# Boundary samples of a modulated convolution chain in three chunks of 43, 43 and 42, in place of four of 32

## The reference, cut to what matters

```python
# x: 128 samples, 64 channels, 1024 positions; style: 128 x 128
for i, typ in enumerate(('same', 'upsample', 'same', 'downsample')):
    s = style @ mod_w[i].T + mod_b[i]
    weight = SCALE * weights[i] * s[:, None, :, None]
    weight = weight * rsqrt(sum(weight**2, over input channels and taps) + EPS)
    # 'same': 3 taps; 'upsample': transposed conv by 2, then the blur 1,3,3,1;
    # 'downsample': the blur, then a conv with stride 2
    out = layer(out, weight, biases[i])
return x + out
```

## Time and profile before

| | us |
|---|---|
| median of 3 runs | 667.52 |
| lowest and highest of the 3 | 664.25, 668.52 |
| the profiled execution | 665.44 |
| its span, first to last instruction | 663.6 |
| mean granted TensorE clock | 0.987 |

### The profile page before, as it was taken

How to read it: one execution, slowest core, us unless ns; L and a number is a source line. 1 busy time by engine, 2 the same in 40 slices (tenths; PEclk the granted TensorE clock), 3 DMA queues, 4 the chain that set the end, 5 groups by cost and what they waited for, 6 DMA issues and landing times.

```text
span 663.6 us, 13288 instructions
## 1 busy us (share of the span) xinstructions
PE 624.9 (94%) x5012; PEld 618.6 (93%) x5012; DVE 534.0 (80%) x800; ACT 431.7 (65%) x713; POOL 230.8 (35%) x246
## 2 busy tenths in 40 slices
PE   5557999999999999999999999999999999999977
PEld 4546999999999999999999999999999999999977
DVE  6898687888888788798888787797888878887941
ACT  3416577686677677776777767666677777666553
POOL 4314324432333333422333344324323343234230
PEclk9988999999999999999999999999999999999989
DMA  5125577767788877777788777777977778778872
GB/s 191 61 63 136 153 205 191 216 200 208 202 213 239 216 182 223 205 196 211 203 232 218 185 220 218 206 192 203 239 197 197 224 209 217 203 189 236 216 197 108
DMA packets 155839, 129.75 MB, mean 196 GB/s; under 512 B 7104, under 2 KB 122304, under 8 KB 155776
## 3 DMA queue, kind: packets, MB, share of 16 engines
q1 hardware_dynamic: 155120, 127.33, 71.2%
q10 hardware_dynamic: 656, 1.57, 0.7%
HBM read 36.41 MB, written 33.75 MB: 106 GB/s over the span
## 4 chain that ended last, share of the span: by engine, by line
PE 76%; DVE 13%; issue 4%; ACT 4%; DMA 1%; POOL 0%; ACTq 0%; DVEq 0%; POOLq 0%
PE py L169 10%; PE py L170 10%; PE py L168 10%; PE pg L168 6%; PE pg L169 6%; PE pg L170 6%; PE ps L168 6%; PE ps L169 6%; PE ps L170 6%; PE pg L173 3%; PE pg L174 3%; DVE pg L667 1%; DVE xl L659 1%; DMA T<-in_a 1%; DVE Q2l L690 1%
## 5 line engine op out<-in xcount | busy, mean ns | idle before, releaser
L169 PE MATMUL py<-xl,W 128*128 128x256 f32 x640 | 182.7, 285 | 0.0
L170 PE MATMUL py<-xh,W 128*128 128x256 f32 x640 | 182.4, 285 | 0.0
L168 PE MATMUL py<-xh,W 128*128 128x256 f32 x640 | 182.1, 285 | 0.1
L614 POOL TENSOR_TENSOR X<-X 128x514 f32<-128x514 f32 x64 | 73.5, 1149 | 218.3 <-DMA X<-in_xin 216.0
L168 PEld LDWEIGHTS py<-xh,W 128*128 128x128 f32 x640 | 127.2, 199 | 0.3 <-ACT py L449 0.3
L170 PEld LDWEIGHTS py<-xh,W 128*128 128x128 f32 x640 | 127.1, 199 | 0.0
L169 PEld LDWEIGHTS py<-xl,W 128*128 128x128 f32 x640 | 126.5, 198 | 0.0
L659 DVE TENSOR_TENSOR xl<-X,xh 128x1548 fp32r<-128x1548 f32 x64 | 114.1, 1782 | 8.7 <-ACT xh L443 8.2
L449 ACT COPY py<-ps 128x512 f32<-128x512 f32 x128 | 73.4, 573 | 69.2 <-PE ps L170 68.8
L168 PE MATMUL ps<-xh,W 128*128 128x256 f32 x384 | 109.6, 285 | 4.2 <-issue 1.9
L169 PE MATMUL ps<-xl,W 128*128 128x256 f32 x384 | 109.2, 284 | 0.0
(11 more groups left out here) (164 smaller groups left out, 1449.9 us busy)
## 6 DMA issues: line engine op xcount, KB each, us to landing
X<-in_xin SPq DMA_DIRECT2D x64, 516.0 KB, 5.4
out<-T SPq DMA_DIRECT2D x64, 512.0 KB, 3.5
W<-W SPq DMA_DIRECT2D x64, 384.0 KB, 4.4
W<-W SPq DMA_DIRECT2D x96, 128.0 KB, 4.3
W<-M SPq DMA_DIRECT2D x96, 128.0 KB, 3.6
W<-W SPq DMA_DIRECT2D x32, 256.0 KB, 4.7
E<-in_ed ACTq DMA_DIRECT2D x1, 768.0 KB, 8.5
XE<-in_xe SPq DMA_DIRECT2D x1, 512.0 KB, 4.8
```

The costliest lines, as they stand in the source:

```text
L168: eng.matmul(o, wh_, rh, start=first, stop=False, skip_group_check=onto)
L169: eng.matmul(o, wh_, rl, start=False, stop=False, skip_group_check=onto)
L170: return eng.matmul(o, wl_, rh, start=False, stop=last, skip_group_check=onto)
L614: pool.tensor_tensor(x[:, :, 3, 0:XW - 1], x[:, :, 0, 1:XW], x[:, :, 1, 0:XW - 1], ALU.subtract)
```

## The change

The chunk size goes from 32 to 43. `chunk(c)` gives the samples of a chunk, 43, 43 and 42, and `NCH` = 3 the number of chunks. Every edge instruction on PE and DVE takes only the first `n` (or `m`) samples of its buffers, which have grown with `EC`. The steps stand in the same places, k-th step of chunk c in groups 8c + 2k and 8c + 2k + 1; groups 24 to 31 now have none.

```diff
-EC = 32
+EC = 43
+def chunk(c):
+    return min(EC, B - c * EC)
+NCH = -(-B // EC)
...
-            sp.wait_ge(s_ed, 5 * (B // EC))
+            sp.wait_ge(s_ed, 5 * NCH)
...
             def edge(c, k):
+                n = chunk(c)
                 pe.wait_ge(s_ed, 5 * c + k + 1)
                 if k == 0:
                     for t in range(3):
-                        m = pe.matmul(pe_[:, 0:6 * EC], E[:, 0, t, :], XS[:, :, t:t + 6], start=t == 0, stop=t == 2)
+                        i = pe.matmul(pe_[:, 0:6 * n], E[:, 0, t, :], XS[:, 0:n, t:t + 6], start=t == 0, stop=t == 2)
...
-                if i == 3 and g % 2 == 0:
+                if i == 3 and g % 2 == 0 and g < 8 * NCH:
                     edge(*divmod(g // 2, 4))
...
-                    link(dve.tensor_scalar(Y[:, :, 1:12], v, BB[:, 0, 1:2], None, ALU.add))
-                    link(tt(Y1[:, :, 0:11], Y[:, :, 1:12], Y[:, :, 0:11], ALU.add))
+                    link(dve.tensor_scalar(Y[:, 0:m, 1:12], v, BB[:, 0, 1:2], None, ALU.add))
+                    link(tt(Y1[:, 0:m, 0:11], Y[:, 0:m, 1:12], Y[:, 0:m, 0:11], ALU.add))
...
-                if i == 2 and g % 2 == 1:
+                if i == 2 and g % 2 == 1 and g < 8 * NCH:
                     c, k = divmod(g // 2, 4)
                     edge(c, k)
-                    if k == 3 and c + 1 < B // EC:
+                    if k == 3 and c + 1 < NCH:
                         edge_in(c + 1)
```

More of the change, by code:

```diff
@@ L359, in edge @@
                     for t in range(3):
-                        m = pe.matmul(pe_[:, 0:6 * EC], E[:, 0, t, :], XS[:, :, t:t + 6], start=t == 0, stop=t == 2)
+                        i = pe.matmul(pe_[:, 0:6 * n], E[:, 0, t, :], XS[:, 0:n, t:t + 6], start=t == 0, stop=t == 2)
                 elif k == 1:
-                    pe.matmul(pe_[:, 0:6 * EC], E[:, 1, 0, :], ZE[:, :, 1:7], start=True, stop=False)
-                    pe.matmul(pe_[:, 0:6 * EC], E[:, 1, 2, :], ZE[:, :, 0:6], start=False, stop=True)
-                    m = pe.matmul(pe_[:, 6 * EC:11 * EC], E[:, 1, 1, :], ZE[:, :, 1:6], start=True, stop=True)
+                    pe.matmul(pe_[:, 0:6 * n], E[:, 1, 0, :], ZE[:, 0:n, 1:7], start=True, stop=False)
+                    pe.matmul(pe_[:, 0:6 * n], E[:, 1, 2, :], ZE[:, 0:n, 0:6], start=False, stop=True)
+                    i = pe.matmul(pe_[:, 6 * n:11 * n], E[:, 1, 1, :], ZE[:, 0:n, 1:6], start=True, stop=True)
                 elif k == 2:
                     for t in range(3):
-                        m = pe.matmul(pe_[:, 0:8 * EC], E[:, 2, t, :], U[:, :, t:t + 8], start=t == 0, stop=t == 2)
+                        i = pe.matmul(pe_[:, 0:8 * n], E[:, 2, t, :], U[:, 0:n, t:t + 8], start=t == 0, stop=t == 2)
                 else:
                     for t in range(3):
-                        m = pe.matmul(pe_[:, 0:3 * EC], E[:, 3, t, :], XB[:, :, t:t + 5:2], start=t == 0, stop=t == 2)
-                m.then_inc(s_e, 1)
+                        i = pe.matmul(pe_[:, 0:3 * n], E[:, 3, t, :], XB[:, 0:n, t:t + 5:2], start=t == 0, stop=t == 2)
+                i.then_inc(s_e, 1)
             for n in ("mwt", "st"):
@@ L719, in edge_in @@
             def edge_in(c):
-                cs = slice(c * EC, (c + 1) * EC)
-                tt(XS, XE[:, cs, :], bc(S[:, 0, cs], 8), ALU.mult).then_inc(s_ed, 1)
+                m = chunk(c)
+                cs = slice(c * EC, c * EC + m)
+                tt(XS[:, 0:m], XE[:, cs, :], bc(S[:, 0, cs], 8), ALU.mult).then_inc(s_ed, 1)
             def edge(c, k):
-                cs = slice(c * EC, (c + 1) * EC)
+                m = chunk(c)
+                cs = slice(c * EC, c * EC + m)
                 dve.wait_ge(s_e, 4 * c + k + 1)
-                got = lambda a, n: pe_[:, a * EC:(a + n) * EC].rearrange("p (b n) -> p b n", n=n)
+                got = lambda a, n: pe_[:, a * m:(a + n) * m].rearrange("p (b n) -> p b n", n=n)
@@ L727, in edge @@
                 if k == 0:
-                    v = Y1[:, :, 0:6]
+                    v = Y1[:, 0:m, 0:6]
                     link(tt(v, got(0, 6), bc(b0z[:, cs], 6), ALU.add))
-                    tt(ZE[:, :, 1:7], v, bc(D10[:, cs], 6), ALU.mult).then_inc(s_ed, 1)
+                    tt(ZE[:, 0:m, 1:7], v, bc(D10[:, cs], 6), ALU.mult).then_inc(s_ed, 1)
                 elif k == 1:
-                    v = Y1[:, :, 0:11]
+                    v = Y1[:, 0:m, 0:11]
                     tt(v[:, :, 0:11:2], got(0, 6), bc(S[:, 1, cs], 6), ALU.mult)
@@ L734, in edge @@
                     link(tt(v[:, :, 1:10:2], got(6, 5), bc(S[:, 1, cs], 5), ALU.mult))
-                    link(dve.tensor_scalar(Y[:, :, 1:12], v, BB[:, 0, 1:2], None, ALU.add))
-                    link(tt(Y1[:, :, 0:11], Y[:, :, 1:12], Y[:, :, 0:11], ALU.add))
-                    link(tt(Y2[:, :, 0:10], Y1[:, :, 1:11], Y1[:, :, 0:10], ALU.add))
-                    link(tt(Y1[:, :, 0:9], Y2[:, :, 1:10], Y2[:, :, 0:9], ALU.add))
-                    dve.scalar_tensor_tensor(out=U[:, :, 1:10], in0=Y1[:, :, 0:9], scalar=0.25, in1=bc(S[:, 2, cs], 9),
+                    link(dve.tensor_scalar(Y[:, 0:m, 1:12], v, BB[:, 0, 1:2], None, ALU.add))
@@ L740, in edge @@
+                    link(tt(Y1[:, 0:m, 0:11], Y[:, 0:m, 1:12], Y[:, 0:m, 0:11], ALU.add))
+                    link(tt(Y2[:, 0:m, 0:10], Y1[:, 0:m, 1:11], Y1[:, 0:m, 0:10], ALU.add))
+                    link(tt(Y1[:, 0:m, 0:9], Y2[:, 0:m, 1:10], Y2[:, 0:m, 0:9], ALU.add))
+                    dve.scalar_tensor_tensor(out=U[:, 0:m, 1:10], in0=Y1[:, 0:m, 0:9], scalar=0.25, in1=bc(S[:, 2, cs], 9),
                                              op0=ALU.mult, op1=ALU.mult).then_inc(s_ed, 1)
                 elif k == 2:
-                    v = Y1[:, :, 0:8]
+                    v = Y1[:, 0:m, 0:8]
@@ L743, in edge @@
                     link(tt(v, got(0, 8), bc(DD[:, 2, cs], 8), ALU.mult))
[L744 to L748, removed]
+                    link(dve.tensor_scalar(HH[:, 0:m, 2:10], v, BB[:, 0, 2:3], None, ALU.add))
@@ L749, in edge @@
+                    link(tt(Y1[:, 0:m, 0:9], HH[:, 0:m, 1:10], HH[:, 0:m, 0:9], ALU.add))
+                    link(tt(Y2[:, 0:m, 0:8], Y1[:, 0:m, 1:9], Y1[:, 0:m, 0:8], ALU.add))
+                    link(tt(Y1[:, 0:m, 0:7], Y2[:, 0:m, 1:8], Y2[:, 0:m, 0:7], ALU.add))
+                    dve.scalar_tensor_tensor(out=XB[:, 0:m], in0=Y1[:, 0:m, 0:7], scalar=0.125, in1=bc(S[:, 3, cs], 7),
                                              op0=ALU.mult, op1=ALU.mult).then_inc(s_ed, 1)
                 else:
-                    v = Y1[:, :, 0:3]
+                    v = Y1[:, 0:m, 0:3]
```

## The result

The changed kernel takes 669.42 us in the median of 20 runs (667.74 to 672.20), the kernel before 666.05 us in 20 runs (664.25 to 668.52). The ratio is 1.0047, with a 95% interval from 1.0037 to 1.0058: by this ratio slower by 3.1 us, between 2.5 and 3.9 (the two medians are 3.4 us apart). The forecast was +1.7 us with a range of 665.0 to 672.0, and "within 1%" as by far the likeliest case. The direction and the class held; the sum came out too small, above the +0.7 to +2.7 us that had 72 in 100.

What follows compares the result with a forecast made beforehand. PE was taken to bound the kernel, DVE costing only where PE waits. PE 0.0, DVE +1.7 and the last part 0 gave +1.7 us, stated as 668.6 us, range 665.0 to 672.0.

Steps and rivals of the forecast that it cites:

- Any time beyond some 2.3 us goes fully to PE: Behind k = 1 and k = 2 steps on DVE: 2.3 us is free room, the rest delays PE one for one.
- growth less the removed wait: DVE's part: k = 1 and k = 2 grow 2.65 us together, less 0.92 for group 27's k = 1 step: +1.73 us.
- the growth of the k = 1 steps of 43 samples: On DVE, 11 more samples add 0.70 us at most, taken as 0.51 since part hides in a wait for POOL.
- the sentence that named it: Odd 43 rows may cost line 735 its double rate: 0.1 us more for each of two k = 1 steps.
- PE's own part: PE's edge steps: k = 0, 1, 2 keep 12.7 us, k = 3 stays 0.66 at its floor; 0.0 us, at most -0.1.
- k = 0 and k = 3 on DVE: These DVE steps stay inside the free room of 2.3 us; k = 3 grows 0.16 and nothing shows.
- The middle of the last part: PE's removed late k = 2 step (1.29 us) shifts it before the `x_low` wait; up to 1.29 lost or 0.85 won, taken as 0.
- the rival in which this step is lost: Last part: `x_low` stays where it is, so the moved k = 2 step gains nothing; +3.0 us, 670; 12 in 100.
- The rival in which fewer instructions win: DVE's 18 removed instructions save 2.8 us of fixed parts; growth hides behind POOL; -1.8 us, 666 or below; 9 in 100.
- Neither buys anything: Last part: PE's k = 3 step in group 30 and DVE's in group 31 lie beside SP's chain; removing them gains nothing.
- one of the prediction's own signs of being wrong: Wrong if the time from 606 us on, less the moved step, changes by over 1.5 us.
- The rival of the falling clock: Longer waits behind k = 1, perhaps k = 2, drop PE to 1.2 GHz: +7 us (674) or +12 us (679); 5 in 100.

Runs made afterwards that it cites:

- the split kernels: DVE's steps k = 1 and k = 2 each cut in two: kernel before (chunks of 32) 661.15 us, 0.9916; changed kernel (43, 43, 42) 661.90 us, 0.9929.
- The 44-row run: Changed kernel with only the tensor_scalar instructions of lines 744 and 753 on 44 rows where a chunk has 43; one run, 667.74 us.
- the kernel without the last step: Kernel before without its very last edge step (k = 3 of the fourth chunk, groups 30 and 31); ratio 0.9998 to before.
- the filler: Changed kernel plus four fp32 matmuls of 336 columns on PE in group 30, results unread; 668.72 us, 1.0035 to before, and 1.0035 when repeated.
- the two shortened ones: Kernel before without its very last edge step, 0.9998 to before; and kernel before without its whole fourth chunk of edge steps, 0.9945.
- the fourth-chunk one: Changed kernel with a fourth chunk of 42 in groups 24 to 31, computing the third chunk's samples twice; 1.0116 to before.
- other k = 3 steps: Changed kernel with PE's k = 3 step reading adjacent columns in group 6, unchanged in 14, 96 columns in 22; one run, 669.65 us.
- the three with a filler: Changed kernel with four extra matmuls in group 30, twice, 1.0035 each; kernel before with DVE steps cut in two plus four 256-column matmuls, 659.85 us, 0.9910.

## Why the prediction was right or wrong

- **Waits behind the steps: right in kind, sized somewhat small.** "Any time beyond some 2.3 us goes fully to PE" held in each of the steps and was used backwards by the split kernels, to 0.1 us. The forecast was 1.43, 1.43 and 1.38 us behind k = 1, measured 1.61, 1.56 and 1.30; and 0.91, 0.91, 0.88 behind k = 2, measured 1.00, 0.90, 0.90. The sum of growth less the removed wait was to be 1.73 us and is 0.74 + 1.27 = 2.01.
- **The term that was mis-sized** is the growth of the k = 1 steps of 43 samples: 0.51 us in the sum, measured 0.69 and 0.65 (the step holds DVE 3.90 us for 3.21 and 3.25), close to the upper end of 0.70 that the prediction took down. It took 0.13 off because line 735 would wait for POOL and hide the growth of lines 733 and 734, and 0.06 because that line would grow at half the price. Neither held. Its successor, line 744, takes 705 and 706 ns, though POOL's row ends 0.32 us before it in one case and 0.50 in the other, so it does not wait for it; the instructions ahead of it push it back by 0.12 us, and it has itself 0.70 us for 0.60. The 44-row run shows that the odd count does this; the sum did without the sentence that named it. With 42 samples the growth was smaller than forecast, 0.30 us for 0.46. The Trainium skill, "VectorE: DVE Perf Modes", section "Mode 2×_2P — use both read ports for one tensor", asks for an outermost dimension that is even, or odd and equal in source and destination. The trace agrees (705 ns with 43 rows, 473 and 573 with 44), if the source of line 744 counts as one run of 473 and its destination as 43 rows. Line 753 has 43 rows on both sides, where this rule expects no loss; it still ends 0.20 us behind POOL's row, as it did before with 0.15, and no run here tells more of it.
- **PE's own part: wrong by 0.37 us.** The step of the prediction that failed is "129 columns cost 0.108 us a pass, still at the floor". The three k = 3 steps cost 0.80 each and not 0.66. k = 0, 1 and 2 kept their sum: the table's rows add up to 12.74 us before and 12.71 after.
- **k = 0 and k = 3 on DVE: right.** No wait behind any of them in 14 profiles.
- **The middle of the last part: right.** The moved step was not lost: PE's wait for `x_low` ahead of sample 118 was 0.52 us and not longer than before (0.85). The same wait was 0.25 to 1.22 us in eleven of the other twelve profiles, of any kernel, and missing in one. So the rival in which this step is lost, at +3.0 us, comes next to the measured 3.1 by luck: its mechanism did not occur. The rival in which fewer instructions win is answered by the middle, which grew although DVE was busy 3.2 us less.
- **The end: wrong in the changed kernel's profiles.** "Neither buys anything" is right, as the kernel without the last step shows (0.0 us, give or take 1.3). That the end could get longer was not considered, and one of the prediction's own signs of being wrong came true: from sample 116 on, behind the moved step, the time grew from 50.85 to 53.00 us, over its 1.5. In both profiles of the changed kernel PE is idle 3.28 us and then runs at 1.2 GHz, which costs 1.47 us in sample 124, and the end is 40.7 and 41.1 us long; with the filler it is 39.0 and 39.1. By the profiles the filler is worth 1.6 to 2.1 us, of which 1.47 is the clock; by the times of all runs less: 1.0047 and 1.0057 without it, 1.0035 twice with it. The mean excess over the kernel before is 3.28 us in the 26 runs without it and 2.34 in the 17 with it, a difference of 0.94 us (95% interval 0.1 to 1.8, by resampling the runs).
- **What makes the wait so long isn't shown.** The missing k = 3 step is some 0.66 us of it. Where the clock falls early, sample 122 takes 4.25 us and more for 2.98, and this fills 1.3 to 1.5 us of the later wait. And the split kernel with chunks of 32, which has the last step, also waited long (2.62 us) and fell late. So the late fall belongs to the changed kernel's profiles, but not to it alone.
- **The rival of the falling clock** was looked for in the wrong place. It set a loss by starts (1.43 us) beside an idle time (1.77 us): of a loss of 1.61 PE was idle 1.34, and the clock stayed at 1.00. The wait of 3.28 us at the end, which no line of the prediction had, was the one that counted.

What stays open: why the clock falls early in one profile and late in another. In all 11 profiles without a filler there is one fall in the end part, either around sample 122 (both of before, the two shortened ones, the fourth-chunk one and the split one with 43), with ends of 38.2 to 39.4 us, or on sample 124 (two of the changed kernel, its two variants with 44 rows and with other k = 3 steps, and the split one with 32), with ends of 40.2 to 42.6. In the three with a filler there is none there, neither early nor late, although the filler stands behind sample 122. The two waits ahead of samples 121 and 122 do not tell the sets apart: the first is 1.46 us in all, the second 1.77 to 2.40 in the early ones and 1.76 to 1.80 in the late ones. Whether the changed kernel falls late more often than the one before was seen in two profiles each and isn't shown beyond that.

## What to carry to other kernels

Price a side task on a busy engine not by its share but by what is queued behind it: here everything up to 2.3 us was free, and everything beyond was paid in full by TensorE, so the same work in fewer, longer portions is dearer, and cutting two of the four kinds of portion in two won 5.6 us where merging lost 3.1. When work is taken out of a stretch in which TensorE waits anyway, look at how long it is then idle and what clock follows. And where a tensor_scalar reads one run and writes rows, try an even number of rows, if need be with one unused: here it took 473 and 573 ns for 705 and 706.

## What the runs showed of the hardware that was not expected

- A tensor_scalar of 43 x 11 elements took 705 ns and two of 44 x 11, with more elements, 573 and 473 ns.
- After 3.28 us without work TensorE soon ran at 1.2 GHz (granted 0.59 and 0.58 over the next 4.1 us, 21 passes for 33); filled up to 0.59 us, it stayed at 2.4 GHz. Single waits of 1.34 us in the middle never lowered it. At the end it fell in six profiles behind waits of 1.46 and 1.77 to 2.40 us, 5 us apart.
- The way from the start to sample 2 takes between 68.6 and 71.8 us in 14 profiles, whatever the kernel. That is 3.2 us between profiles, where the runs of one kernel differ by some 4, and it is why differences of 1 us are read from the middle stretch and not from the time.
